# Attention units of one head by two key tiles by half of the queries, with one PSUM bank for value products and three for jobs

## What is computed

```python
x_flat = x.reshape(B, C, N).transpose(0, 2, 1)      # N = 1024 tokens, C = 192
qkv = x_flat @ qkv_w.T + qkv_b                      # 8 heads of 24
q = _l2norm(q); k = _l2norm(k)
attn = softmax(einsum('bhnd,bhmd->bhnm', q, k) * temperature)
out = einsum('bhnm,bhmd->bhnd', attn, v)
out = out.transpose(0, 2, 1, 3).reshape(B, N, C) @ proj_w.T + proj_b
```

## Time and profile before

| What | us |
|---|---|
| median of three runs | 2734.44 |
| lowest and highest run | 2732.74, 2734.46 |
| the profiled execution's own time | 2724.55 |
| its span, first to last instruction | 2722.8 |

### The profile page before, as it was taken

How to read it: one execution, slowest core, us unless ns; L and a number is a source line. 1 busy time by engine, 2 the same in 40 slices (tenths; PEclk the granted TensorE clock), 3 DMA queues, 4 the chain that set the end, 5 groups by cost and what they waited for, 6 DMA issues and landing times. The chain is left out here.

```text
span 2722.8 us, 58859 instructions
## 1 busy us (share of the span) xinstructions
PE 2467.2 (91%) x18693; PEld 1299.5 (48%) x18693; DVE 1672.2 (61%) x4869; ACT 1780.4 (65%) x2228; POOL 1422.4 (52%) x1137
## 2 busy tenths in 40 slices
PE   4699999999989989999999974999999999999975
PEld 3333333333333333333333322777777777777755
DVE  5556766766766776686676655555555555555522
ACT  2587777777778777777777852555555555555542
POOL 3334435534543543554454333677777777777750
PEclk8799999999999999999999986999999999999987
DMA  4121112112112111211211353444444444444419
GB/s 100 51 59 36 49 48 59 48 43 62 49 48 51 54 43 49 59 48 42 54 50 52 79 175 135 154 159 171 158 160 171 157 160 173 155 160 174 154 73 340
DMA packets 160582, 276.56 MB, mean 102 GB/s; under 512 B 21828, under 2 KB 129844, under 8 KB 150884
## 3 DMA queue, kind: packets, MB, share of 16 engines
q1 hardware_dynamic: 141908, 245.43, 27.9%
q0 software_dynamic: 13392, 27.97, 2.8%
q10 hardware_dynamic: 5056, 0.42, 0.2%
HBM read 174.07 MB, written 49.69 MB: 82 GB/s over the span
## 5 line engine op out<-in xcount | busy, mean ns | idle before, releaser
L802 ACT ACTIVATE probs<-ps_s 128x1024 f32<-128x1024 f32 x1024 | 1012.1, 1023 | 282.5 <-PE ps_s L701 275.0
L1374 POOL TENSOR_TENSOR h_split<-h_f,h_split 128x512 f16<-128x512 f32 x444 | 552.0, 1244 | 237.2 <-ACT h_f L1351 230.0
L1347 ACT ACTIVATE h_split<-ps_h,packs 128x512 f16<-128x512 f32 x444 | 305.2, 687 | 391.2 <-PE ps_h L1301 391.0
L1301 PE MATMUL ps_h<-m_xn_t,packs 128*128 128x512 f16 x2220 | 553.6, 380 | 0.5 <-DVE m_xn_t L1436 0.5
L714 PE MATMUL ps_o<-probs,v_aug 128*32 128x512 f32 x4096 | 549.4, 609 | 0.4 <-ACT probs L802 0.4
L1068 POOL TENSOR_TENSOR inv_norm<-sumsq,minus_half 128x16 f32<-128x16 f32 x128 | 378.0, 2953 | 305.7 <-DVE sumsq L1011 305.7
L1315 PE MATMUL ps_y<-packs,h_split 128*128 128x192 f16 x5328 | 511.9, 245 | 0.6 <-POOL h_split L1374 0.6
L1315 PEld LDWEIGHTS ps_y<-packs,h_split 128*128 128x128 f16 x5328 | 453.1, 97 | 105.1 <-POOL h_split L1374 1.1
L701 PE MATMUL ps_s<-stacks_odd 98*128 98x512 f16 x1024 | 300.9, 385 | 16.6 <-DMA stacks_odd<-heads 9.9
L701 PE MATMUL ps_s<-even 98*128 98x512 f16 x1024 | 299.5, 383 | 11.3 <-ACT probs L802 5.7
L1351 ACT ACTIVATE h_f<-ps_h,packs 128x512 f32<-128x512 f32 x444 | 302.0, 680 | 0.0
(11 more groups left out here) (213 smaller groups left out, 2805.2 us busy)
## 6 DMA issues: line engine op xcount, KB each, us to landing
packs<-expert_pack SPq DMA_DIRECT2D x74, 1635.0 KB, 6.9
even<-heads SPq DMA_DIRECT2D x192, 96.0 KB, 2.3
stacks_odd<-heads SPq DMA_DIRECT2D x192, 96.0 KB, 2.4
tile_rows<-sorted_rows SPq DMA_DIRECT2D x37, 400.0 KB, 6.6
tokens<-in_x_dram SPq DMA_DIRECT2D x17, 768.0 KB, 5.4
y_in<-y_tokens SPq DMA_DIRECT2D x16, 768.0 KB, 8.7
out_dram<-y_out SPq DMA_DIRECT2D x16, 768.0 KB, 6.7
even<-heads SPq DMA_DIRECT2D x128, 48.0 KB
```

What stands on the lines that cost most here:

```text
L802: act.activation(probs[:, u % PRING, :], ps_s[:, u % 2, :, :].rearrange("p f n -> p (f n)"), ACT.Exp).then_inc(s_probs, 1)
L1301: mm = pe.matmul(ps_h[:, n % HBUF, :], w1(par, slot, w, k), xn_t[0:rows_k, par, c, :], start=(i == 0), stop=(i == 4))
L1347: act.activation(h_split[:, n % HSPLIT, 0, :], ps_h[:, n % HBUF, :], ACT.Gelu, bias=bias1(par, slot, k), scale=1.0 / WSCALE)
L1374: pool.tensor_tensor(h_split[:, n % HSPLIT, 1, :], h_f32[:, n % HBUF, :], h_split[:, n % HSPLIT, 0, :], ALU.subtract).then_inc(s_h, 1)
```

## The change

A unit becomes one head by two key tiles by half of the queries (512). The 64 units are four phases of 16 (`PHASE`): head group, then half of the queries, then pair of key tiles, then head. Sizes and numbers of instructions of an image stay: two score products of 512 columns per unit, and the value products of a set come in two calls, now one for each key tile (`i`), both into the one bank of `ps_o`. A sum over 8 key tiles is complete after 16 units. The calls stand at units 5 and 7 of a set's four (counted from its start), in the first set of a phase at 6 and 7. There are still four takes per image, now at units 4, 20, 36 and 52, each followed two units later by a new sum in the same bank. `ps_m` gets the freed bank as a third, and a job waits for the job three before it. Unit 0 needs only half of the queries' replicas and the first pair of key tiles; each pair of key tiles is waited for when it is first read (units 4, 8, 12), the other half of the queries at unit 16.

```diff
-PV_LAG = GH + 1
-PV_AT = range(1, UNITS, 2)
-TAKE_AT = (2, 4)
+PHASE = UNITS // 4
+
+PV_UNITS = [GH * p + at for p in range(UNITS // GH) for at in ((6, 7) if p % (PHASE // GH) == 0 else (5, 7))]
+TAKE_AT = 4
+BANKS = 3
...
-    ps_o = ctx.enter_context(nc.psum_tensor("ps_o", [P, 2, HALF], F32))
-    ps_m = ctx.enter_context(nc.psum_tensor("ps_m", [P, 2, HALF], F32))
+    ps_o = ctx.enter_context(nc.psum_tensor("ps_o", [P, HALF], F32))
+    ps_m = ctx.enter_context(nc.psum_tensor("ps_m", [P, BANKS, HALF], F32))
...
+    def bank_of(img, par, n):
+        return n % 6 if isinstance(img, int) and img == B else (n + par) % BANKS
+
+    def wait_bank(pe, img, par, n):
+
+        if n >= BANKS:
+            wait_taken(pe, img, n - BANKS)
+        elif not (isinstance(img, int) and img == -1):
+            of_bank = [i for i in range(len(jobs_of(img - 1))) if bank_of(img - 1, 1 - par, i) == bank_of(img, par, n)]
+            wait_taken(pe, img - 1, of_bank[-1])
...
-        g, m, j = u // (UNITS // 2), u % (UNITS // 2) // GH, u % GH
+
+        g, f, pair, j = u // (2 * PHASE), u // PHASE % 2, u % PHASE // GH, u % GH
         h = g * GH + j
         if u == 0:
             pe.wait_ge(s_ones, 2 + 2 * 16)
             for r in range(2):
+                pe.wait_ge(s_rep_q[r], 2 * REP_Q * img + REP_Q)
+        if u == PHASE:
+            for r in range(2):
                 pe.wait_ge(s_rep_q[r], 2 * REP_Q * (img + 1))
-                pe.wait_ge(s_rep_k[r], 2 * REP_K * (img + 1) - REP_K * r)
-        if g == 0 and m == NT - 2 and j == 0:
-            pe.wait_ge(s_rep_k[1], 2 * REP_K * (img + 1))
+        if u < PHASE and j == 0:
+            pe.wait_ge(s_rep_k[pair % 2], 2 * REP_K * img + REP_K * (pair // 2 + 1))
...
-        p, f = k // 2, k % 2
-        g, m = p // NT, p % NT
-        if f == 0:
+        p, i = k // 2, k % 2
+        g, m = p // NT, p % (PHASE // GH) * 2 + i
+        if i == 0:
             pe.wait_ge(s_probs, UNITS * img + GH * p + GH)
-        if m == 0 and not (isinstance(img, int) and img == 0 and g == 0):
-            pe.wait_ge(s_o, 4 * img + 2 * g + f - 1)
+        if m == 0 and not (isinstance(img, int) and img == 0 and p == 0):
+            pe.wait_ge(s_o, 4 * img + p // (PHASE // GH))
...
-        elif not (isinstance(img, int) and img == -1 and n < 2):
-            wait_taken(pe, img, n - 2)
+        else:
+            wait_bank(pe, img, par, n)
...
-            if u in TAKE_AT and has_post(img):
-                take_o(dve, img - 1, 1 - par, 1, TAKE_AT.index(u))
-            if u - UNITS // 2 in TAKE_AT and attend:
-                take_o(dve, img, par, 0, TAKE_AT.index(u - UNITS // 2))
+            if u == TAKE_AT and has_post(img):
+                take_o(dve, img - 1, 1 - par, 1, 1)
+            elif u % PHASE == TAKE_AT and u > TAKE_AT and attend:
+                phase = u // PHASE - 1
+                take_o(dve, img, par, phase // 2, phase % 2)
```

More of the change, by code:

```diff
@@ L545, in _ @@
             for k in range(2):
-                mm = pe.matmul(ps_o[:, 0, 0:NE], ones[0:HC, :], bias_gx[:, k, :], start=(k == 0), stop=(k == 1))
+                mm = pe.matmul(ps_o[:, 0:NE], ones[0:HC, :], bias_gx[:, k, :], start=(k == 0), stop=(k == 1))
             mm.then_inc(s_wg, 1)
@@ L594, in _ @@
             dve.wait_ge(s_wg, 5)
-            st.now(dve.tensor_copy(const_gx[:, :], ps_o[:, 0, 0:NE]))
+            st.now(dve.tensor_copy(const_gx[:, :], ps_o[:, 0:NE]))
             dve.wait_ge(s_wt_free, n)
@@ L693, in scores @@
             for r in range(2):
+                pe.wait_ge(s_rep_q[r], 2 * REP_Q * img + REP_Q)
+        if u == PHASE:
+            for r in range(2):
                 pe.wait_ge(s_rep_q[r], 2 * REP_Q * (img + 1))
-                pe.wait_ge(s_rep_k[r], 2 * REP_K * (img + 1) - REP_K * r)
-        if g == 0 and m == NT - 2 and j == 0:
-            pe.wait_ge(s_rep_k[1], 2 * REP_K * (img + 1))
+        if u < PHASE and j == 0:
+            pe.wait_ge(s_rep_k[pair % 2], 2 * REP_K * img + REP_K * (pair // 2 + 1))
         if not (isinstance(img, int) and UNITS * img + u < 2):
             pe.wait_ge(s_probs, UNITS * img + (u - 1))
-        for f in range(2):
-            mm = pe.matmul(ps_s[:, u % 2, f, :], stacks[par][:, 1, h, m * P:(m + 1) * P],
+        for i in range(2):
+            m = 2 * pair + i
+            mm = pe.matmul(ps_s[:, u % 2, i, :], stacks[par][:, 1, h, m * P:(m + 1) * P],
                            stacks[par][:, 0, h, f * HALF:(f + 1) * HALF], start=True, stop=True)
@@ L786, in pe_image @@
                 scores(pe, img, par, u)
-            if u in PV_AT and u >= PV_LAG and attend:
-                pv(pe, img, par, (u - PV_LAG) // 2)
-            elif u in PV_AT and u < PV_LAG and has_post(img):
-                pv(pe, img - 1, 1 - par, PVS + (u - PV_LAG) // 2)
+            if u in PV_UNITS and attend:
+                pv(pe, img, par, PV_UNITS.index(u))
+            elif u + UNITS in PV_UNITS and has_post(img):
+                pv(pe, img - 1, 1 - par, PV_UNITS.index(u + UNITS))
             for job in jobs_at(img, u):
@@ L825, in take_o @@
     def take_o(dve, img, par, g, f):
-        dve.wait_ge(s_pv, PVS * img + PVS // 2 * (g + 1) - 1 + f)
-        dve.tensor_copy(o_sb[:, par, g, f * HALF:(f + 1) * HALF], ps_o[:, f, :]).then_inc(s_o, 1)
+        dve.wait_ge(s_pv, PVS * img + PVS // 4 * (2 * g + f + 1))
+        dve.tensor_copy(o_sb[:, par, g, f * HALF:(f + 1) * HALF], ps_o[:, :]).then_inc(s_o, 1)
     def dve_job(dve, img, par, n, job, pre, post, route):
```

7 lines of the change are left out of this document (3 added, 4 removed).

## The result

| What | before, us | changed, us |
|---|---|---|
| median of four runs | 2733.59 | 2692.19 |
| lowest and highest run | 2732.49, 2734.46 | 2690.4, 2693.47 |
| the profiled execution's own time | 2724.55 | 2691.2 |
| its span | 2722.8 | 2689.5 |

The ratio of the two medians is 0.9848, 95% interval 0.9831 to 0.9865: 1.5% faster. Between the two profiled executions 33.3 us of span went, between the medians 41.4: the profiled execution of before lay 9 us under its median, that of the changed kernel 1 us under. No trace shows those 8 us, and I don't explain them.

The account below looks back on a forecast made before the run. PE was taken to bound the kernel, with only its idle time to shrink: 30 us in images 1 to 14, 5 at the start, 2 in image 15, together 37, from 2734.4 to 2697.4 us; range 2664 to 2722.

Parts of the forecast that it names:

- Units 19 to 23: Waits of 11.4 us for job banks go but turn into a take wait of about 1.3 us at unit 22; nothing won.
- Unit 24: With three banks a2 waits less for an evacuation; 1.1 us per image won, 13.2 over twelve.
- Units 30 to 42: Job-bank waits of a3, c1 and b3, 17.7 us over twelve images, mostly go; 16 us won.
- Units 1 to 8: x3's wait for a bank goes; 0.6 us per image won, 7.2 over twelve, bounds 0 and 9.3.
- Units 47 to 55: The take comes too late for unit 54; 0.9 us per image lost, 10.8 over twelve, a6's 3.9 won and lost.
- Busy time: PE's busy time stays the same, with the same number of products of the same shapes; only idle time can change.
- Gains given back: Rival: the delayed norms chain through POOL doesn't recover, losing gains at units 24 and 38; 2722 us, chance 0.13.
- Takes hidden: Rival: DVE reaches units 20 and 52 sooner, so all 58.7 us of bank waits go; 2656 us, chance 0.12.
- Slower: Rival: takes at all four phase starts end 1.0 us later than read, stalling PE and starving ACT; 2753 us, chance 0.07.
- Replicas: Image 0's first product no longer waits 5.44 us for the last queries' transfer; 5 us won.
- The gap at loop turns: PE's 2.5 us gap is the jump back and stays; rival, a replica wait: 12.5 us more go, 2685 us, chance 0.06.
- Image 15: One more job can pass each of three waits for c's evacuation, behind scatters; 2 us won, from 0 to 5.

Follow-up runs that it names:

- e3: The changed kernel with an unused second read of the value bank, some 0.7 us on DVE, ahead of the take of unit 20: 2715.79 us, ratio 0.9919 to before.
- e4: The changed kernel with the take of unit 20 moved behind unit 19's evacuations and that of unit 52 to the end of unit 50: 2679.06 us, ratio 0.9794.
- e7: e4 with the first value calls of the phases beginning at units 16 and 48 sooner, at 21 and 23, 53 and 55: 2669.71 us, ratio 0.9774.
- e11: e8 with the take of the second phase at the head of unit 19's list, ahead of the evacuations of u1 and a0: 2653.04 us, ratio 0.9723.
- e8: e7 with tile 0's scaling of heads moved from unit 19 to unit 20, behind v1's evacuation and norms: 2664.91 us, ratio 0.9761.
- e1: The changed kernel with two job banks again, keeping new units, single value bank, takes and eased replica waits: 2763.58 us, ratio 1.0089 to before.
- e9: The changed kernel run again unchanged, on another chip: 2688.87 us, ratio 0.9855 to the kernel before.
- e10: e2 run once more, beside the changed kernel on the same chip: 2695.23 us, ratio 0.9878 to the kernel before.
- e5: The changed kernel with two value banks, used in turn by phase, and two job banks; takes and calls stay: 2749.19 us, ratio 1.0062 to before.
- e6: The changed kernel with an unused second read of the value bank, some 0.7 us, ahead of the take of unit 36: 2699.78 us, ratio 0.9882.
- e2: The changed kernel with unit 0 waiting for all queries and all but the last pair of key tiles, as before: 2707.86 us, ratio 0.9896.

## Why the prediction was right, point by point

- **The sum.** 25.6 us were forecast for twelve images and 27.6 measured; 37 in all, with 33.3 in the spans and 41.4 in the medians. The time, 2692.19, is 5.2 under the forecast. The method held: walk the engine that bounds unit by unit through the new order, and ask at each wait removed who is late next. The size of the total hides errors that cancel, and is in part luck: the prediction took all of it from idle time, which fell by 17.7 us in the twelve images and not by 25.6, and busy time, put at nothing, gave 9.9. The errors of the single terms follow.
- **Units 19 to 23: right.** The stretch was to stay as long and took 2.5 us more over twelve images, 1.6 of them in image 9 behind the fall of the clock. The wait for the take is 1.3 us at unit 22 in eleven of the twelve images and 1.0 in one, and in image 10 PE is at unit 23 within 0.2 us of its old time. e3 and e4 confirm who decides: a longer take lengthens this wait by as much, an earlier one removes it.
- **Unit 24: right, a bit small.** 15.9 for 13.2. n3 then waited 0.22 us (0.25 forecast).
- **Units 30 to 42: right, small.** 20.4 for 16.
- **Units 1 to 8: too large.** 2.5 for 7.2. I took 0.6 us net per image for won; 0.2 were. The small wait for ACT at unit 6 that I had foreseen is there (2.6 over twelve), and one for the take (1.8), of which I had said that there would be none.
- **Units 47 to 55: the right cost, the wrong cause.** 10.8 - 6.5 + 3.8 = 8.1 for 10.8. I named the take as the larger wait and ACT as the smaller. In the changed kernel's image 10 the take ends 2.4 us after the scores of unit 52 start, for 2.6 in my working, and ACT isn't earlier; so the wait of unit 54 is ACT's, 6.5 us, and the take's is 0.5. e7 shows it: with the calls apart, it goes.
- **Busy time: the step that failed.** "Its busy time doesn't change" was wrong by 9.9 us. A product ahead of a wait is shown 0.60 us long, and where none waits the next starts 0.44 after it, so each stall is some 0.16 us longer than its bracket says. Before, a6 at unit 47 had a gap of 0.33 in brackets:

```profile
1130.97 0.61 PE L757 MATMUL ps_m<-ident,heads 128*96 128x128 f16 x8
1131.90 0.44 PE L763 MATMUL ps_m<-ident,o_sb 128*128 128x128 f32 x2 [0.33 <-DVE heads L853]
1132.18 1.03 PE L701 MATMUL ps_s<-even 98*128 98x512 f16 x4
```

  Units 47 to 48 became 0.54 us shorter per image (6.5 over twelve). PE's idle times of over 0.15 us fell from 155 to 126, and 29 times 0.16 is 4.7 us, half of the 9.9; stalls too short for a bracket may be the other half. Counted from the start of each product to the next one's (or to its end, where PE then stands), 9.6 of the 9.9 us are in two kinds of product: the transposes of queries and keys (L757, 50.1 to 45.1 us) and the products of 292 columns (66.2 to 61.6). PE stood behind one of them 71 times before and 16 times now. That is argued from the two traces; no run isolates it.
- **Exponentials.** I called it wrong if those waits grew by more than 5 us, and they grew by 11: the waits of units 6 and 54 above and short ones behind. ACT didn't become the bound (876.5 of 1139.5 us busy), but it is next in line at single places.
- **Evacuations: right.** The four lines named, L756, L779, L784 and L761, wait 9.2 us for evacuations, for under 10 forecast. The products of L737, which I hadn't named, wait another 2.3, and 3.2 for their data. e4 to e11 show that such small waits are where removed waits go.
- **Gains given back: didn't come.** The chain through POOL recovered, as unit 24 shows.
- **Takes hidden: didn't come.** It needed DVE earlier; e11 puts the take earlier by hand and is 13 us over twelve images better than e8 (which had 10 us more at the low clock), so a part of this rival's gain existed, but not in this order of DVE's list.
- **Slower: near in e1.** The mechanism, DVE late at the first call, is real: 0.7 us on one of four takes cost 21.0 us in the twelve images (e3). I had priced a microsecond of it by its length alone, 12 us per place in twelve images. By length e3's wait is 7.2 us; the term that I left out is the clock that falls behind the gap, the other 14.
- **Replicas: right.** The wait of 5.44 us of the earlier trace rows is gone and the first product starts at 97.78, 1.8 later than forecast because the preparation ended later, its last q at 96.92 for 94.60 before. In e9 it ended at 96.60. e10 puts the term at 4.9 us by the first product and 6.4 by the medians, for my 5; from the last q to the first product it is 5.7 (6.60 for 0.85).

```profile
96.92 1.06 PE L773 MATMUL ps_m<-ident,heads 128*96 128x128 f16 x8 [5.75 <-DVE heads L1044]
97.78 1.91 PE L717 MATMUL ps_s<-even 98*128 98x512 f16 x4
```

- **The gap at loop turns: right.** With the wait for late replicas out of unit 0, the gap is still 2.2 to 2.7 us, five times, and the trace now puts it down to nothing:

```profile
1129.62 1.03 PE L717 MATMUL ps_s<-stacks_odd 98*128 98x512 f16 x4 [2.22 <-issue]
```

```profile
L1172 PEldq COMPARE_BRANCH  x6: 83/3480/4027, 551.6 to 1505.3; - x6
```

  The median of the branch is 3480 ns (3604 before). The Trainium skill's 108 ns (Advanced Engine Details and Errata, Control Flow Timing) don't describe this jump back; the row decides.
- **Image 15: wrong sign.** 2 us were to be won, and the end became 2.0 us longer. The bank wait of 9.9 us didn't shrink but moved one job on, from L768 to the projection:

```profile
PE ps_m L737 <- DVE rows L908: 10.6, 3, 6.9
```

  DVE is held there by scatters, and one more job ahead of it doesn't bring it sooner. The step that failed was to count a job that may pass as time won: 2 us forecast, 2.0 lost.

Weighed against the Trainium skill's rule to rotate groups through banks so that evacuation overlaps computing (Perfetto Trace Analysis, Optimizing Tensor Performance, Matmuls): for jobs the runs agree, 66 us for the third bank. For the value products rotation is worth 7 us at most (e5 against e1, with two job banks), and where takes, calls and norms stand in the lists was worth more: with e4, e7, e8 and e11, 0.9848 to 0.9723 without another bank.

## What to carry to other kernels

A wait for a bank has two handles, the number of banks and the place of the evacuation in the evacuating engine's list; give the bank to the many short jobs, and move the one long copy ahead of the work that nobody on PE waits for. Walk the new order on the engine that bounds and on the one that feeds it, and price a wait from the chain it ends in; where two waits end within 0.3 us of one another, name both. A gap of 1.3 to 1.9 us on PE can cost twice its length or more, because the clock may fall behind it; behind the half-microsecond gaps of e4 and e11 it didn't. Before a small difference is explained, count the stretches at the low clock in both traces.

## What the runs showed of the hardware

- **The clock after a gap.** Inside the images the granted clock fell to 0.50 (1.2 GHz) at units 63 to 1 around the loop turns (gaps of 2.1 to 2.8 us) and at unit 21 or 22 of the kernels in which PE stood 1.3 to 1.9 us there. With 1.9 us it fell in eight (e3), ten (e1) and seven (e5) images of twelve; with 1.3 us in one (the changed kernel), none (e9, the same program), one (e6), two (e10) and four (e2, the same program as e10). So the gap alone doesn't decide it, and what does stays open. The one of the changed kernel:

```profile
968.72 1.92 PE L730 MATMUL ps_o<-probs,v_aug 128*32 128x512 f32 x8 [1.31 <-DVE o_sb L844]
```

  Eight products of 1.06 us took 1.92. A stretch at unit 22 cost 2.1 us of an image in e3 and 0.3 in e10: e10's two images made 1.3 us of it good again in units 24 to 43. That the clock can make a gap cost more than twice its length is worked out from e3: 7 us of added waits, 21 of time.
- **Runs of one kernel on different chips.** The changed kernel's ratio was 0.9848 and 0.9855, and e2 and e10, the same program, differ by 12.6 us in median and 0.18% in ratio. The preparation of image 0, which e2 to e4, e6 and e7 leave as in the changed kernel, reached its last q between 93.24 us (e4) and 96.94 (e7); on one chip it was 93.24 in e4 and 96.18 in e2. So a term of 5 us needs runs side by side, and the trace must show it in its own place.
